# Last stage of an attention and soft-mixture kernel: an earlier wait for a load, and one lower half moved from VectorE to Pool

## The reference

```python
# x: (2, 2048, 256); 64 experts with 32 slots each = 2048 slots; soft mixture on x3 = layernorm(x)
x = x + layernorm(attention(layernorm(x)))            # linear attention without a softmax
...
logits = einsum('bmd,dnp->bmnp', x, phi)
dispatch = softmax(logits, axis=0)                    # over the batch, which is 2
combine = softmax(logits.reshape(b, m, n * p), axis=-1).reshape(b, m, n, p)
slots = einsum('bmd,bmnp->bnpd', x, dispatch)
y = einsum('bnpd,nde->bnpe', slots, W) + bias
out = einsum('bnpd,bmnp->bmd', y, combine)
# result: x + layernorm(out)
```

## Time and profile before

| | |
|---|---|
| median of 3 runs | 654.41 us (654.32 to 654.46) |
| profiled execution | 654.63 us, of which the profile's span is 652.4 us |
| busy in the span: PE, DVE, ACT, POOL | 97%, 67%, 56%, 36% |

### The profile page before, as it was taken

How to read it: one execution, slowest core, us unless ns; L and a number is a source line. 1 busy time by engine, 2 the same in 40 slices (tenths; PEclk the granted TensorE clock), 3 DMA queues, 4 the chain that set the end, 5 groups by cost and what they waited for, 6 DMA issues and landing times.

```text
span 652.4 us, 15309 instructions
## 1 busy us (share of the span) xinstructions
PE 630.5 (97%) x5353; PEld 395.8 (61%) x5353; DVE 437.7 (67%) x859; ACT 367.3 (56%) x712; POOL 237.5 (36%) x416
## 2 busy tenths in 40 slices
PE   8999999999999999999999987799999999999996
PEld 7898645445444444444444455577777777777775
DVE  4978898733333423234333588999999988888885
ACT  5666876742333323324345295777777777777773
POOL 5365887710000000000000052555555555555555
PEclk9999999999999999999999999999999999999999
DMA  8910032325544544454455521132222222222201
GB/s 270 400 61 1 9 70 49 66 61 154 137 133 127 137 133 128 133 133 118 104 161 132 155 74 65 41 127 92 91 92 90 89 88 88 88 88 88 88 16 34
DMA packets 70167, 68.72 MB, mean 105 GB/s; under 512 B 6258, under 2 KB 66675, under 8 KB 67827
## 3 DMA queue, kind: packets, MB, share of 16 engines
q1 hardware_dynamic: 67792, 66.09, 34.4%
q10 hardware_dynamic: 2338, 2.16, 0.9%
HBM read 43.32 MB, written 23.07 MB: 102 GB/s over the span
## 4 chain that ended last, share of the span: by engine, by line
PE 75%; DVE 10%; POOL 5%; ACT 5%; issue 4%; DMA 1%; POOLq 0%; SPq 0%; DVEq 0%; ACTq 0%
PE psL L1589 23%; PE psM L1576 11%; PE psL L1708 10%; PE psM L1726 7%; PE psM L1727 6%; PE psM L1730 6%; PE psM L1606 3%; POOL small L489 2%; PE psL L1474 2%; ACT r_xn L868 1%; DVE small L1278 1%; DVE r_xn L1297 1%; ACT r L868 1%; DMA xres<-in_x 1%; PE psM L1532 1%
## 5 line engine op out<-in xcount | busy, mean ns | idle before, releaser
L1589 PE MATMUL psL<-r,r_xn 128*128 128x512 f16 x768 | 176.4, 379 | 0.8 <-DVE r L1119 0.8
L1589 PEld LDWEIGHTS psL<-r,r_xn 128*128 128x128 f16 x768 | 73.3, 98 | 91.6 <-issue 6.8
L1117 DVE TENSOR_SCALAR r<-r 128x512 f16<-128x512 f32 x64 | 29.0, 453 | 96.3 <-ACT r L758 96.3
L1576 PE MATMUL psM<-phs,xx 128*128 128x512 f16 (+1 forms) x384 | 93.2, 379 | 0.0
L758 ACT ACTIVATE r<-psM,small 128x512 f32<-128x512 f32 x64 | 43.6, 682 | 75.9 <-PE psM L1576 75.1
L576 POOL MEMSET r_xn<- 128x16 f16 x1 | 0.2, 173 | 234.9 <-PE psL L1589 234.9
L1708 PE MATMUL psL<-phs,r 128*32 128x512 f16 x1344 | 75.1, 379 | 2.0 <-DMA r<-xx 1.5
L1576 PEld LDWEIGHTS psM<-phs,xx 128*128 128x128 f16 x384 | 37.3, 98 | 44.8 <-issue 0.7
L868 ACT ACTIVATE r<-psL,small 128x512 f32<-128x512 f32 x60 | 41.9, 776 | 31.3 <-DVE small L1305 22.0
L489 POOL TENSOR_TENSOR small<-small,epst 128x2 f32<-128x2 f32 (+3 forms) x75 | 56.9, 759 | 6.2
L1708 PEld LDWEIGHTS psL<-phs,r 128*32 128x32 f16 x1344 | 34.6, 97 | 38.3 <-issue 2.6
(11 more groups left out here) (208 smaller groups left out, 1292.7 us busy)
## 6 DMA issues: line engine op xcount, KB each, us to landing
logit_difference<-r SPq DMA_DIRECT2D x256, 64.0 KB, 1.8
xx<-logit_difference SPq DMA_DIRECT2D x16, 1024.0 KB, 5.2
r<-in_ffn_w SPq DMA_DIRECT2D x15, 1024.0 KB, 5.5
out<-r SPq DMA_DIRECT2D x32, 128.0 KB, 1.7
xres<-in_x SPq DMA_DIRECT2D x7, 512.0 KB, 11.0
r<-in_phi SPq DMA_DIRECT2D x1, 2048.0 KB, 18.1
expert_bias<-r ACTq DMA_DIRECT2D x1, 2048.0 KB, 20.0
r<-expert_bias SPq DMA_DIRECT2D x16, 128.0 KB, 2.2
```

Of the source, the lines that this page charges most:

```text
L1576: ins = mm(bk[j % 2][:, :].rearrange("p (q m) -> p q m", q=EP), xxT[:, 1, j, hx, k, :], phw[:, hp, k, :, bass.ds(nb, 1), :].rearrange("p q ...
L1589: ins = mm(psL[:, i * 512:(i + 1) * 512], x3n[:, b, j, hx, k * P:(k + 1) * P], thl[:, j % 2, hs, :], start=(j == 0 and hx + hs == 0), stop ...
```

## The change

It has two parts.

First, on SP: `loads(j)` waits for `l_done` of the tile before (4 per tile) before it loads `x1_now`, where it waited for `m0_masked`; the load of `dB` behind it still waits for `m0_masked`.

Second, the first lower half of batch 0 in tile 1 moves from VectorE (where it was part of `comb_dve(2, False, True)`) to Pool, between `mean(1, 0)` and `lo_second(1)`, with a semaphore of its own, `el0_pool`. `lows_ready` on TensorE and `turns` on VectorE wait for it in that one tile, and the values awaited of `el_ready[0]` are one lower from there on.

```diff
             def loads(j):
 
+                wait_apart(sp, l_done, 4 * j)
+                load_x1(j)
                 wait_apart(sp, m0_masked, j)
-                load_x1(j)
                 load_d(j)
...
             lo_second(0)
             mean(1, 0)
+            pool.wait_ge(eh_ready[0], 3)
+            nc.gpsimd.tensor_tensor(eT0[:, 1, 0:8, :].rearrange("p t m -> p (t m)"), ET0[:, 0:1024],
+                                    eT0[:, 0, 0:8, :].rearrange("p t m -> p (t m)"), ALU.subtract).then_inc(el0_pool, 1)
             lo_second(1)
             mean(0, 1)
...
-            def turns(b, j, first=False):
+            def turns(b, j, first=False, third=False):
...
                 else:
-                    dve.wait_ge(el_ready[0], j)
+                    if third:
+                        dve.wait_ge(el0_pool, 1)
+                    else:
+                        dve.wait_ge(el_ready[0], 1 if first else j - 1)
                     dve.wait_ge(el_pool, j)
...
                 add_max(j, 0)
                 add_max(j, 1)
-                if third:
-                    lo(0, j - 1, 0)
-                elif not first:
+                if not first and not third:
                     exp_bias(0, j, FOLD[1], m1_folded, m1_ready)
                 add_max(j, 2)
                 add_max(j, 3)
...
-            def lows_ready(b, j, half, last):
+            def lows_ready(b, j, half, last, second):
 
                 if b:
                     pe.wait_ge(el_ready[1], 2 * j + half - 1)
                 elif half and last:
-                    pe.wait_ge(el_ready[0], NJ + 1)
+                    pe.wait_ge(el_ready[0], NJ)
+                elif half:
+                    pe.wait_ge(el_pool, j + 1)
+                elif second:
+                    pe.wait_ge(el0_pool, 1)
                 else:
-                    pe.wait_ge(el_pool if half else el_ready[0], j + 1)
+                    pe.wait_ge(el_ready[0], j)
```

More of the change, by code:

```diff
@@ L308, in build @@
         eh_ready, el_ready = [sem(f"eh_ready{b}") for b in range(B)], [sem(f"el_ready{b}") for b in range(B)]
-        el_pool = sem("el_pool")
+        el_pool, el0_pool = sem("el_pool"), sem("el0_pool")
         comb_done, ys_ready = sem("comb_done"), sem("ys_ready")
@@ L1332, in comb_dve @@
                 turn(1, j, 1)
-                turns(0, j)
+                turns(0, j, first, third)
                 turn(0, j, 0)
@@ L1795, in combine @@
                     if t % 8 == 0:
-                        lows_ready(b, j, t // 8, not more)
+                        lows_ready(b, j, t // 8, not more, second)
                     ins = low(b, t, acc, t == NT - 1)
```

## The result

The changed kernel takes 656.88 us (median of 6, 656.37 to 657.56); the kernel before took 654.26 beside it (6 runs). The ratio is 1.0041, 95% interval 1.0028 to 1.0054: slower by 2.6 us. The forecast was 654.7, no difference that can be told; the first rival, Pool first at the port, had 656.7 and 17%.

The account below looks back on a forecast made before the run. TensorE, with VectorE equally critical at tile 3, was taken as the bound. VectorE 1.94 us late less 1.64 saved gives + 0.30, put on the median 654.41: 654.7 us, range 653.7 to 656.9.

Parts of the forecast that it names:

- the first rival: Near 411 us Pool gets in first and both VectorE scalings are held; + 2.3, 656.7 us; chance 17%.
- What it collides with: Pool's new half against VectorE's two scalings of y near 411: they alternate, VectorE 1.94 us late, net + 0.30.
- the paragraph on the Trainium skill: Port pair held by whichever starts first; VectorE, 0.02 us ahead, holds on to L1358, sum + 0.30, otherwise + 2.3.
- the rows at 69.11: Trace rows of the kernel before: Pool started 0.05 us ahead of VectorE's L1148, yet Pool waited; cited against Pool first.
- The rows at 87.27: Trace rows of the kernel before: Pool was 0.06 us ahead and VectorE waited; cited for Pool first.
- The exclusion and the alternation: VectorE's scalings and Pool's instructions exclude each other, and a waiting Pool instruction gets its turn between two of VectorE's.
- The rival's own sum: Pool first near 411: L1360 ends 3.96 late, less 1.64 gives 2.32 at tile 3's maxima; 656.7 us, chance 17%.
- its own case: VectorE's first scaling near 411 goes first, the second is held; + 0.30 us at tile 3's fold; 68%.
- the moved load gives nothing: x1 load for tile 3 stays behind the store delayed by Pool; logits at 422.35 to 422.65, against 422.48.
- VectorE keeps its turn: Near 411 both scalings run before Pool's new half, which waits until 412.44; 654.2 us, chance 8%.
- small instructions that might collide once more: Small Pool and VectorE instructions, moved against each other, set the upper end, 655.3 us, of the forecast case.
- The clock, which the prediction put aside: TensorE's granted clock is 1.00 in the windows, so it was said to play no part.

Follow-up runs that it names:

- e4: Changed kernel with Pool's new half held until the addition in front of VectorE's first scaling is done; 654.40 us, 654.49 before.
- e2: Changed kernel with SP's order of before, only the lower half moved to Pool; 657.01 us, 654.49 before.
- e1: Kernel before with only SP's part of the change, the earlier load of x1; 654.69 us, 654.49 before.
- e6: Kernel before with the load of x1 for tile 3 put ahead of the first store; 654.36 us, 654.36 before.
- e3: Changed kernel with Pool's new half held until both scalings of y on VectorE are done; 655.48 us, 654.49 before.
- e10: Changed kernel with one wait on an already reached semaphore ahead of Pool's new half; 656.70 us, 654.48 before.
- e11: Changed kernel with three waits on an already reached semaphore ahead of Pool's new half; 656.98 us, 654.48 before.
- e5: As e3, with the load of x1 for tile 3 ahead of the first store; 655.64 us, 654.48 before.

## Why the prediction was wrong

**The step that failed** is the one under "What it collides with" and in the paragraph on the Trainium skill: that VectorE, recorded 0.02 us ahead, "holds on to L1358". The recorded offset was right (0.02 to 0.03 us in four traces); the owner of the port was the other. What the runs showed in its place: Pool first, L1363 (the old L1358) 2.71 us long and L1365 2.60, so VectorE 3.83 us late, where the forecast had 1.94. The rival had been given 17% for it, with the rows at 69.11 weighed against it, in which Pool was 0.05 us ahead and second. Those are a tensor_scalar of two elements on Pool and a tensor_tensor on VectorE; here it is a tensor_tensor on Pool and a tensor_scalar on VectorE. The rows at 87.27, with a tensor_tensor on Pool (and another kind of instruction on VectorE), pointed the right way. So a recorded start doesn't tell who asked first, and a row of one pair of instructions doesn't settle another pair; with 0.02 us between them the two cases should have had about the same chance, and the rows with the same Pool instruction the greater weight.

Why Pool got in ahead of a scaling recorded before it stays open. One reading is that VectorE counts only from the end of its predecessor, which overlaps the scaling in the record: 410.17 + 0.41 = 410.58, against Pool's 410.53. It fits e4 (predecessor's end 411.15, Pool 411.30, VectorE first), e2 (411.27, 411.22, Pool first), and in the kernel before the rows at 87.27 (87.42, 87.27, Pool first) and at 597 (L1254's predecessor ends at 597.09, Pool's L602 starts at 597.13 and takes 1.55 us for 0.56: VectorE first). It doesn't fit 69.11, where the predecessor ends at 69.25 and VectorE is first all the same. No run tested it.

**What held.** The exclusion and the alternation: measured in the changed kernel (the two halves of Pool and the two scalings take turns) and in e4. The rival's own sum: L1360 3.96 us late, measured 3.83; + 2.3 at the fold of tile 3, measured + 2.26; 656.7, measured 656.88. That the last two agree so well is in part luck, as the sum has no term for the clock (below): the profiled execution is the shortest of the six (656.37), and its own fall of the clock came early, where it shortened the wait for the scaled y. The forecast's sum for its own case: e4, + 0.23 for + 0.30. That a stall of TensorE is worth nothing while VectorE is as critical at tile 3: e1 and e6. That the moved load gives nothing: e1, though not for the reason given, that Pool's work keeps the load late; in e1 the stall goes and the time stays.

**What was mis-sized.** "VectorE keeps its turn" was priced at 654.2, and e3, which forces it, showed that this case has another wait, of the 128x16 mask for 1.8 us, which the sum had left out: Pool's second half is then in the way at 415. The forecast wrote of small instructions that might collide once more, and its range for them ended 0.6 us above its own time; one alone cost 1.8. A held scaling was taken to end 0.62 us behind Pool (0.75 less 0.13); the row cited for it, 0.27 us for 0.42, gives 0.15 less, and in the changed kernel it is 0.55 both times. That is nearly the whole difference of 3.96 and 3.83. The clock, which the prediction put aside, seems to add something where TensorE is left idle long: in e2, e10 and e11, which had waits of 3.6 us for the scaled y, the clock was 0.52, 0.52 and 0.80 in the window from 418 to 421, and fold to fold is 2.52 to 2.85, not 2.26.

## What to carry to other kernels

Before a half of elementwise work is moved from VectorE to Pool, list what VectorE does in the time that it will take there. Here its scalings, its 128x16 mask and its 128x4 bias waited until Pool's instruction had ended, while its reductions from PSUM beside the same instruction did not (2.48 us for four at 412.51 in e3, and 2.48 at 492.68 in the kernel before, where Pool does no such half). A waiting Pool instruction breaks up a pair of VectorE's, and who came first was worth 2.0 us (the changed kernel against e4). The move paid once VectorE's scalings were put elsewhere, into a gap that it had anyway, and Pool's halves were put around its mask. And where two engines are late at the same point, a stall taken from one is worth nothing until the other is relieved.

## What the runs showed of the hardware

A tensor_tensor on VectorE of 16 elements per partition took 1.96 us for 0.18 behind a Pool instruction of 2.12 us: that it is small doesn't shorten the wait. The kernel before has such a wait in the very stretch that decides, between its two maxima of tile 3, behind Pool's L581 (431.73 to 433.86):

```profile
432.56 1.32 DVE L1305 TENSOR_SCALAR small<-small 128x4 f32<-128x4 f32 x1
```

It takes 0.23 us at 437.73, so 1.1 us are lost there ahead of the column maxima at 435.13, and VectorE has hardly a gap in between. What moving Pool's half away from it would give, no run tried.

The granted clock fell in some executions and not in others of the same kernel: its mean over a run is 0.993 to 1.00 in the runs of the kernel before, but for one stray. In e1 it was 0.74, 0.50 and 0.62 in the windows from 397 to 406, after stalls that all the kernels have there, and the 96 products of the logits took 7.40 us for 5.36. It cost e1 nothing: its fold to fold is 39.30, as TensorE then had its waits for VectorE to give. In the timeline of e1:

```profile
401.11 7.40 PE L1709 MATMUL psL<-phs,r 128*32 128x512 f16 x96 [0.24 <-ACT r L869]
```

The changed kernel's profiled execution has such a fall there too (0.55, 0.50 and 0.81 in the same windows); it met the wait for the scaled y, which is 2.94 us in it and 3.64 in e2, where the clock held until 415. In e5, besides one at 397, a fall came at 418, where TensorE had nothing left to give: fold to fold is + 1.43, against + 0.12 in e3, whose VectorE and Pool do the same and whose clock held.
